# Sixteen chunks of a recurrence, written out in a row in place of a loop of three turns

## What is computed

```
def step(S, xs):
    q_t, k_t, v_t, a_t, b_t = xs
    Sk = jnp.einsum('bhvk,bhk->bhv', S, k_t)
    S = a_t[..., None] * S - (b_t[..., None] * (Sk - v_t))[..., None] * k_t[:, :, None, :]
    o_t = jnp.einsum('bhvk,bhk->bhv', S, q_t)
    return (S, o_t)
```

```
o = (o - mu) * lax.rsqrt(var + 1e-05) * ln_g + ln_b
g = jax.nn.sigmoid(x @ Wg.T).reshape(B_, T_, H, DV)
o = (o * g).reshape(B_, T_, H * DV)
return o @ Wo.T
```

## Time and profile before

| | us |
|---|---|
| median of three runs | 2372.58 |
| lowest, highest | 2368.91, 2380.48 |
| profiled execution, its time | 2377.0 |
| its span | 2375.3 |
| TensorE products / VectorE / ScalarE / GpSimd busy | 2071.1 / 1897.3 / 1239.1 / 522.0 |

### The profile page before, as it was taken

How to read it: one execution, slowest core, us unless ns; L and a number is a source line. 1 busy time by engine, 2 the same in 40 slices (tenths; PEclk the granted TensorE clock), 3 DMA queues, 4 the chain that set the end, 5 groups by cost and what they waited for, 6 DMA issues and landing times.

```text
span 2375.3 us, 61546 instructions
## 1 busy us (share of the span) xinstructions
PE 2071.1 (87%) x21890; PEld 1575.9 (66%) x21890; DVE 1897.3 (80%) x4382; ACT 1239.1 (52%) x2692; POOL 522.0 (22%) x577
## 2 busy tenths in 40 slices
PE   6999999999994788888888888888887887866999
PEld 4444788888884667667667766666766766742666
DVE  4222699999995788988888988888988988977776
ACT  4000577777772556555555655655655545523332
POOL 0000044444442112221221212222221211221000
PEclk9999999999996899999898989989998988877999
DMA  7000177777779566666666566566666556566440
GB/s 267 9 9 9 62 255 255 255 255 255 264 264 347 182 235 205 214 200 224 208 202 229 188 213 224 192 212 225 205 212 216 194 171 198 187 227 265 178 160 19
DMA packets 229473, 468.45 MB, mean 197 GB/s; under 512 B 48432, under 2 KB 172328, under 8 KB 199640
## 3 DMA queue, kind: packets, MB, share of 16 engines
q1 hardware_dynamic: 222920, 450.91, 54.8%
q10 hardware_dynamic: 6240, 13.86, 1.6%
q0 software_dynamic: 48, 0.16, 0.0%
HBM read 316.36 MB, written 149.57 MB: 196 GB/s over the span
## 4 chain that ended last, share of the span: by engine, by line
PE 49%; DVE 27%; issue 14%; ACT 7%; DMA 2%; DVEq 1%; ACTq 1%; POOL 0%; POOLq 0%; SPq 0%
DVE arena L1081 10%; PE PS L1520 8%; PE PS L1680 5%; PE PS L1596 4%; PE PS L1534 4%; PE PS L1506 4%; PE PS L1387 3%; PE PS L1460 3%; DVE arena L1172 3%; PE PS L1559 3%; ACT arena L856 2%; PE PS L1547 2%; DVE arena L1187 2%; DVE arena L1180 2%; PE PS L1410 2%
## 5 line engine op out<-in xcount | busy, mean ns | idle before, releaser
L1410 PE MATMUL PS<-arena 128*128 x2048 | 463.7, 386 | 1.8 <-DVEq L1066 1.0
L1081 DVE SCALAR_TENSOR_TENSOR arena<-PS,SM,arena 128x256 f32<-128x256 f32 x1152 | 452.9, 478 | 15.5 <-ACT arena L725 15.5
L1410 PEld LDWEIGHTS PS<-arena 128*128 128x128 f32 x2048 | 383.4, 188 | 82.1 <-DVE arena L1081 6.5
L1520 PE MATMUL PS<-arena 128*128 128x128 f32 x1920 | 317.4, 315 | 39.2 <-ACT arena L864 37.5
L1520 PEld LDWEIGHTS PS<-arena 128*128 128x128 f32 x1920 | 267.6, 216 | 77.8 <-ACT arena L864 56.4
L856 ACT ACTIVATE arena<-arena 128x128 f32<-128x128 f32 x960 | 306.8, 396 | 0.0
L631 POOL TENSOR_TENSOR arena<-arena 128x256 f32<-128x256 f32 x128 | 114.6, 895 | 873.2 <-DVE arena L1187 873.2
L725 ACT ACTIVATE arena<-PS,SM 128x256 f32<-128x256 f32 x384 | 209.8, 565 | 88.9 <-PE PS L1410 84.1
L1506 PE MATMUL PS<-ident,arena 128*128 128x128 f32 x960 | 172.7, 309 | 28.3 <-ACT arena L856 27.1
L1126 DVE TENSOR_TENSOR arena<-arena,PS 128x512 f32<-128x512 f32 x192 | 127.5, 685 | 75.4 <-PE PS L1559 71.6
L873 ACT COPY arena<-PS 128x256 f32<-128x256 f32 x240 | 89.6, 373 | 187.2 <-PE PS L1520 184.3
(11 more groups left out here) (135 smaller groups left out, 3170.9 us busy)
## 6 DMA issues: line engine op xcount, KB each, us to landing
arena<-g_d SPq DMA_DIRECT2D x126, 1024.0 KB, 5.6
arena<-vas_d SPq DMA_DIRECT2D x124, 384.0 KB, 3.3
vas_d<-arena SPq DMA_DIRECT2D x32, 1024.0 KB, 11.4
kq_d<-arena SPq DMA_DIRECT2D x8, 4096.0 KB, 11.5
arena<-kq_d SPq DMA_DIRECT2D x14, 2048.0 KB, 8.2
arena<-beta_d SPq DMA_DIRECT2D x8, 2048.0 KB, 9.2
kb_d<-arena SPq DMA_DIRECT2D x8, 2048.0 KB, 10.3
vas_d<-arena SPq DMA_DIRECT2D x8, 2048.0 KB, 12.5
```

The costliest lines, as they stand in the source:

```text
L1081: nc.vector.scalar_tensor_tensor(acc, raw[:, :, i:i + PT_], CW[:, w, i, hh:hh + 1], acc, ALU.mult, ALU.add).then_inc(job_free if i == TAPS ...
L1410: ins = mm(dst.rearrange("p (b n) -> p b n", b=B), W4[:, w, kt, DH * h:DH * (h + 1)], XNT[:, kt, :, bass.ds(c * PT_ + (HALO - halo), halo ...
L1520: ins = mm(bank(7)[:, 128 * gi:128 * (gi + 1)].rearrange("v (l x) -> v l x", l=NB), STR[:, s % 2, gi, :], KQ[d][:, :, p0:p0 + 2].rearrange ...
```

## The change

In `chunks` the loop over three turns with four chunks each goes, and all sixteen chunks are written out by a Python loop, on each of the five engines. What each chunk does stays the same. The number of a chunk, and with it every value that is waited for and every address in DRAM, becomes a constant. `divmod(n, 4)` gives the same pair `(i, q)` for chunks 0 to 11, and `n // 2` the same count per buffer.

```diff
         def chunks(engine, chunk):
 
-            with engine.Fori(0, NS // 4 - 1) as i:
-                for q in range(4):
-                    chunk(i * 4 + q, i * 2 + q // 2, q % 2, True, True, (i, q))
-            for c in range(2):
-                chunk(NS - 4 + c, NS // 2 - 2, c, True, True, None)
-            chunk(NS - 2, NS // 2 - 1, 0, True, False, None)
-            chunk(NS - 1, NS // 2 - 1, 1, False, False, None)
+            for n in range(NS):
+                chunk(n, n // 2, n % 2, n < NS - 1, n < NS - 2, divmod(n, 4) if n < NS - 4 else None)
```

## The result

The changed kernel is slower by a little: 2389.28 us in the median of 20 runs against 2379.12 of 20 runs of the kernel before. The ratio is 1.0042, with a 95% interval from 1.0025 to 1.006, so +10 us, between 6 and 14. The forecast was +5.2 us and "the same within 0.5%" as the likeliest. The sign, the range and the likeliest outcome held, though the interval reaches beyond 0.5%; the forecast size was about half of what came. The forecast of 2378 us stood on 2372.6 us for the kernel before. In these runs that kernel took 2379.1, so the difference is what can be compared: it would put the changed kernel at 2383 on the forecast's base.

What follows compares the result with a forecast made beforehand. No engine was simply the bound (TensorE busy 87%, VectorE 80%); hand-over between engines counted. A 9.6 us loss by waits less 4.4 by branches, +5.2 on 2372.6, gave 2378 us; range 2366 to 2391.

Steps and rivals of the forecast that it cites:

- the same within 0.5%: Whole kernel: time between 2360.7 and 2384.5 us, no change that a measurement can tell; chance 0.77.
- loss by VectorE's waits: VectorE in chunks 0 to 11: waits written out cost more than looped ones; 9.6 us, bounds 3.6 and 20.4.
- gain by TensorE's branches: TensorE at the loop's two back edges: two taken branches go; 4.4 us gained, upper bound 6.35.
- constants in place of register values: VectorE's waits before lines 1187 and 1126: the constant form adds 1.7 us of idle time a chunk.
- size of the loss on the path: Twelve looped chunks: 0.8 us of the added 1.7 exposed in each, the rest swallowed by waits for TensorE; 9.6 us.
- reason for not taking the 1.95 us: Written-out chunk at 1823.85, 1.95 us over the loop's: 2.15 put down to missing early gate tiles and TensorE's lower clock.
- Rival A: VectorE's waits: nothing is covered, TensorE idles more and gets a lower clock; +17.3 us, 2390 us; chance 0.17.
- a branch costs VectorE 56 ns: VectorE at line 329: a branch takes 56 ns, against a median of 4060 on TensorE's sequencer.
- Code at no cost: Code fetch: straight code needs the same 16 KB blocks as the loop, 164 on one queue; zero taken.
- Chunks 4 and 8 about 1.4 shorter: Sign in the profile after: the chunks behind the two back edges, each about 1.4 us shorter.
- The nine others 0.8 longer: Sign in the profile after: chunks 1 to 3, 5 to 7 and 9 to 11 some 0.8 us longer on average.

Runs made afterwards that it cites:

- the version with all but TensorE: The changed kernel with the loop of three turns kept on TensorE alone; 1.0064 (1.0045 to 1.0082) to the kernel before.
- the swapped version: The changed kernel with VectorE's two waits in the other order in sub, add(0) and level_sub; 0.9951 and 0.9975 to the kernel before.
- the loop against the straight version with the good order: Kernel before with waits of sub, add(0), level_sub reordered, 0.9989, against the changed kernel with the same three reordered, 0.9951 and 0.9975.

## Why the prediction was right, and where it was not

*The two terms and their signs were right.* A loss by VectorE's waits and a smaller gain by TensorE's branches were forecast, and both appear in the trace where they were expected. The loss was seen before by reading the one chunk already written out against a looped one. What the prediction named as its reason, constants in place of register values, is not the cause as such: with constants in the good order the idle time is 6.4 us, as in the loop. The cause is which of two waits the instruction carries.

*The size of the loss on the path was too small.* This is the term that failed: 0.8 us a chunk, 9.6 in all. VectorE alone written out gave +16 us, and the version with all but TensorE +15, both with the branches still in. So the term is about 15 us, or 1.3 a chunk of the 1.7 that were counted. I had reckoned that VectorE's waits for TensorE swallow what is added ahead of them. They hardly did. Over chunks 1 to 11 the wait for TensorE before line 1126 was 41.2 us before and 33.4 after, and at the chunks' heads it went from 36.1 to 43.7:

```profile
L1126 DVE TENSOR_TENSOR arena<-arena,PS 128x512 f32<-128x512 f32 x132 | 87.6, 685 | 42.7 <-PE PS L1559 41.2
L1115 DVE TENSOR_TENSOR arena<-arena,PS 128x256 f32<-128x256 f32 x176 | 61.1, 415 | 36.1 <-PE PS L1470 36.1
```

```profile
L1121 DVE TENSOR_TENSOR arena<-arena,PS 128x512 f32<-128x512 f32 x132 | 87.7, 685 | 39.4 <-PE PS L1554 33.4
L1110 DVE TENSOR_TENSOR arena<-arena,PS 128x256 f32<-128x256 f32 x177 | 61.6, 415 | 43.7 <-PE PS L1465 43.7
```

The branches have to be taken out of both. Of the 41.2 us, 6.35 are the two waits that TensorE's branches caused. And at the two back edges VectorE itself did nothing for a while, which the profile puts to "issue"; once the branch is gone, this time counts as a wait for TensorE:

```profile
1119.64 0.28 DVE L1164 TENSOR_TENSOR arena<-arena 128x64 f32<-128x64 f32 x1 [4.28 <-issue]
...
1473.06 0.28 DVE L1164 TENSOR_TENSOR arena<-arena 128x64 f32<-128x64 f32 x1 [3.48 <-issue]
```

So the comparison is 41.2 - 6.35 + 36.1 + 7.8 = 78.8 us before against 33.4 + 43.7 = 77.1 after: the waits shrank by 1.7 us, where some 17 had been added. These are two single executions, and the sum holds only to a few us. Why the rest is not swallowed is argued, not shown: TensorE's work in a block starts from what VectorE and ScalarE handed it one block earlier, so that a later VectorE makes a later TensorE, and the wait stays.

*The reason for not taking the 1.95 us was wrong.* I explained 2.15 us of the written-out chunk by the missing gate tile. But chunks 1 and 3 of the changed kernel have the wait with the tile, and two of three chunks of the swapped version lack it without. The low clock before it is real (0.82 and 0.85); what brings it there is not shown. The plain difference of the chunks, 1.95, would not have been a good guide either: the term came out at 1.3, between it and the 0.8 that I took. Rival A's mechanism, no cover, is three quarters of the truth, for 1.3 of its 1.7 us were exposed; that TensorE's clock had a part in it was not tested. Its 2390 us did not come because of the last quarter and because the branches seem to have given some us back.

*The gain by the branches was likely about right.* 4.4 was taken. By the middles, all but TensorE against all gives 4 to 5, and the loop against the straight version with the good order 3 to 9; no two versions run beside each other have intervals that part. TensorE alone written out did not show it; why not stays open. The one long wait for code seen in its trace would do it in that execution, but a single profile says nothing of the other runs. One reading was wrong: that a branch costs VectorE 56 ns. That is the instruction alone; VectorE's next one came 4.28 and 3.48 us late, as shown above. It was covered, as the prediction said, since VectorE then still waited 1.41 and 0.68 us for TensorE's carried products.

*Code at no cost was only half right.* The number of blocks is nearly as forecast, 157 against 164. But straight code has stalls of its own, of which I had said that no row shows them. In the changed kernel those of 0.9 us or more, at 844, 1310, 1688 and 1835 us, sum up to 5.9 us of TensorE's time. The kernel before has some too, 5.0 us apart from its branches. Over all traces the sum is 3.8 to 7.4 us in the eight with TensorE written out (mean 5.6), and 0 to 5.0 in the five with its loop (mean 2.5, branches apart). So some 3 us of TensorE's time may be the change's share; whether they reach the kernel's time is not shown.

*The single chunks.* "Chunks 4 and 8 about 1.4 shorter": 88.82 and 88.83 against 89.69 and 88.13, so 0.9 shorter and 0.7 longer. "The nine others 0.8 longer": 1066.34 - 96.18 - 88.82 - 88.83 = 792.51, or 88.06 each against 87.38, 0.68 longer. That the last comes near the forecast 0.8 is luck: three unchanged chunks differ by 4.9 us, 1.6 each.

## What to carry to other kernels

Where an instruction waits for two semaphores, look at which wait the instruction carries itself: it should be the one that comes last, and the satisfied one should stand ahead. Here 256 instructions, each 0.07 us late, made the kernel some 16 us slower, more than two loop branches of 4 us each. Writing out a loop can change this order without a change in the source of the instruction. If some turns of a loop are written out already, compare a chunk of each kind by the idle time before each line. Count the added idle time as exposed, and take something off for cover only by a reason that has itself been tested.

## What the runs showed of the chip that I had not expected

In `sub`, a wait in the sequencer ahead of the VectorE instruction, ended by that engine's previous instruction, leaves 104 ns between the two; the same wait carried by the instruction leaves 34 ns. TensorE sometimes stands still for 0.9 to 3.5 us in straight code, until 2.2 to 2.4 us after a transfer of its code has begun; in 28 of 28 cases this was at the same place of a block of 256 instructions. 128 more instructions ahead moved these places with the code. A branch back over four chunks took 4.0 to 5.0 us on TensorE, in the five versions that have it. On VectorE it took 0.06, though VectorE, too, then did nothing for 3.2 to 4.3 us before its next instruction.
